# An attention and mixture-of-experts layer on one core: a unit's near tables written by one transfer and read by one, in place of six of half units

## What is computed

```python
scores = jnp.einsum('bhqd,bhkd->bhqk', q, k) / scale
rel = build_relative_position(S, S, BUCKETS, MAX_REL)        # log buckets of q - k
c2p = jnp.take_along_axis(jnp.einsum('bhqd,hpd->bhqp', q, pos_k), clip(rel + ATT_SPAN), axis=-1)
p2c = jnp.take_along_axis(jnp.einsum('bhkd,hpd->bhkp', k, pos_k), clip(-rel + ATT_SPAN), axis=-1)
scores = scores + (c2p + swapaxes(p2c, -1, -2)) / scale
probs = jax.nn.softmax(scores, axis=-1)
ctx = jnp.einsum('bhqk,bhkd->bhqd', probs, v)
```

## Time and profile before

| | us |
|---|---|
| median of 3 runs | 1870.73 (1870.19 to 1876.4) |
| the profiled execution's own time | 1863.67 |
| its span, first to last instruction | 1861.8 |
| PE busy | 1708.2 (92%) |
| DVE busy | 1417.6 (76%) |
| ACT busy | 1163.0 (62%) |
| POOL busy | 1057.3 (57%) |
| mean granted TensorE clock | 0.919 of full speed |

### The profile page before, as it was taken

How to read it: one execution, slowest core, us unless ns; L and a number is a source line. 1 busy time by engine, 2 the same in 40 slices (tenths; PEclk the granted TensorE clock), 3 DMA queues, 4 the chain that set the end, 5 groups by cost and what they waited for, 6 DMA issues and landing times. The chain is left out here.

```text
span 1861.8 us, 41287 instructions
## 1 busy us (share of the span) xinstructions
PE 1708.2 (92%) x13752; PEld 1164.0 (63%) x13752; DVE 1417.6 (76%) x4111; ACT 1163.0 (62%) x2784; POOL 1057.3 (57%) x1260
## 2 busy tenths in 40 slices
PE   7953899999999999999999999999869967999997
PEld 4531565666666666666666666666435656999996
DVE  4751898999999999999999999999534453555553
ACT  6843577788887888888888888787613441222221
POOL 0002777777777777877778777788214321333332
PEclk9985899999999999999999999999955566999998
DMA  5976787878778887788887877877065424666662
GB/s 152 302 259 214 250 277 261 278 256 284 263 257 296 267 276 262 268 285 267 278 276 253 288 260 264 274 262 244 19 169 182 139 74 137 208 189 201 201 198 68
DMA packets 297313, 426.33 MB, mean 229 GB/s; under 512 B 35773, under 2 KB 238545, under 8 KB 297008
## 3 DMA queue, kind: packets, MB, share of 16 engines
q1 hardware_dynamic: 285764, 393.28, 64.7%
q10 hardware_dynamic: 7596, 21.10, 3.6%
q0 software_dynamic: 3744, 9.31, 1.4%
HBM read 245.85 MB, written 178.05 MB: 228 GB/s over the span
## 5 line engine op out<-in xcount | busy, mean ns | idle before, releaser
L839 ACT ACTIVATE t_probsT<-t_flip 128x512 f32<-128x512 f32 x1024 | 626.0, 614 | 201.8 <-PE t_flip L735 148.0
L785 DVE TENSOR_REDUCE t_most<-t_scores 128x1 f32<-128x640 f32 (+1 forms) x512 | 435.0, 850 | 82.1 <-PE t_scores L712 78.8
L804 DVE TENSOR_SCALAR t_band<-t_band,t_top 128x384 f32<-128x384 f32 (+1 forms) x512 | 413.9, 809 | 0.0
L749 PE MATMUL t_sum_ps<-t_probsT,t_vals 128*32 128x256 f32 x4096 | 327.7, 392 | 0.2 <-ACT t_probsT L839 0.2
L831 ACT COPY t_table<-t_table_ps 128x388 f32<-128x388 f32 x512 | 247.9, 484 | 56.3 <-issue 29.0
L916 POOL TENSOR_TENSOR t_near<-t_near,masks 128x768 f32<-128x768 f32 (+1 forms) x128 | 273.5, 2137 | 0.0
L789 DVE CUSTOM_DVE_ANT_0 t_band<-t_scores,t_near 128x384 f32<-128x384 f32 (+1 forms) x512 | 261.6, 511 | 0.0
L735 PE MATMUL t_flip<-masks,t_band 128*128 128x128 f32 x1408 | 261.1, 274 | 0.0
L712 PE MATMUL t_scores<-masks,t_near 128*128 128x128 f32 x1408 | 241.8, 275 | 5.0 <-POOLq L919 5.0
L705 PE MATMUL t_scores<-t_afters,t_quests 105*128 105x256 bf16 (+3 forms) x1024 | 244.0, 288 | 1.3 <-DVE t_most L789 1.3
L900 POOL TENSOR_TENSOR t_near<-t_near,masks 128x384 f32<-128x384 f32 (+1 forms) x128 | 147.1, 1149 | 124.1 <-DMA t_near<-skew_d 117.5
(11 more groups left out here) (194 smaller groups left out, 2670.2 us busy)
## 6 DMA issues: line engine op xcount, KB each, us to landing
skew_d<-t_table SPq DMA_DIRECT2D x128, 1024.0 KB, 9.3
t_near<-skew_d SPq DMA_DIRECT2D x128, 640.0 KB, 8.1
t_near<-skew_d SPq DMA_DIRECT2D x128, 384.0 KB, 7.3
e_w<-in_L_ffn_W_dram ACTq DMA_DIRECT2D x39, 512.0 KB
e_w<-in_L_ffn_W_dram SPq DMA_DIRECT2D x39, 512.0 KB
split_d<-p_part SPq DMA_DIRECT2D x32, 384.0 KB, 3.3
t_afters<-split_d SPq DMA_DIRECT2D x128, 96.0 KB
t_quests<-split_d SPq DMA_DIRECT2D x128, 96.0 KB
```

The lines of the kernel that those rows point to most:

```text
L749: last = nc.tensor.matmul(sum_ps[32 * g:32 * g + 32, 0:2 * P], vals[b % 2][:, j, h * VDIM:h * VDIM + 32], probsT[s % 3][:, g * 2 * P:(g + ...
L785: nc.vector.tensor_reduce(most[:, c, 1:2], out[:, wide:S], AX.X, ALU.max)
L804: nc.vector.tensor_scalar(band[n % 2][:, t, 0:wide], band[n % 2][:, t, 0:wide], top[n % 2][:, t:t + 1], None, ALU.subtract).then_inc(level ...
L839: nc.scalar.activation(probsT[s % 3][:, half * 512:(half + 1) * 512], flip_ps[half][:, :], ACT.Exp, scale=SCALE).then_inc(expd, 1)
```

## The change

The two halves of a unit's tables become one piece: one write of 2048 KB, one read of 2048 KB. `table` in SBUF is laid out so that a partition's 16 KB are contiguous, as they are in HBM. In SP's loop the read of unit u+1 comes first, then the loads, then the write of unit u+2. The read waits for the whole unit of two before (`scored`, `seen`) and for the whole write. `edge` waits for the one read; its steps are issued later in the loop. `load_vals(0)` and the clearing of `spent` semaphores move to later rounds of SP's loop. The constant rows go out in three transfers over all six buffers, on one semaphore.

```diff
-            def skew_write(n, h):
-                sp.wait_ge(table_kept, n * QT + 4 * h + 4)
+            def skew_write(n):
+                sp.wait_ge(table_kept, n * QT + QT)
                 if n >= 2:
-                    sp.wait_ge(skew_in[n % 2][0], 16 * 2 * (n // 2))
-                    sp.wait_ge(skew_in[n % 2][1], 16 * 2 * (n // 2))
-                sp.dma_start(view(skew_d, n % 2 * (P * PITCH) + h * 4 * SPOT + 1, [[PITCH, P], [TABLE, 2], [1, 4 * SPOT]]),
-                             table[n % 2][:, h, :, :, :].rearrange("p a u v -> p a (u v)")).then_inc(skew_out[n % 2][h], 16)
-
-            def skew_read(n, h):
+                    sp.wait_ge(skew_in[n % 2], 16 * (n // 2))
+                sp.dma_start(view(skew_d, n % 2 * (P * PITCH) + 1, [[PITCH, P], [1, PITCH]]),
+                             table[n % 2][:, :, :, :].rearrange("p a u v -> p (a u v)")).then_inc(skew_out[n % 2], 16)
+
+            def skew_read(n):
                 if n >= 2:
-                    sp.wait_ge(scored, (n - 2) * QT + 4 * h + 4)
-                    sp.wait_ge(seen, (n - 2) * QT + 4 * h + 4)
-                sp.wait_ge(skew_out[n % 2][h], 16 * (n // 2 + 1))
-                lo, hi = PIECES[h]
-                for tab in range(2):
-                    sp.dma_start(near[n % 2][:, tab, lo:hi, P:W3],
-                                 view(skew_d, n % 2 * (P * PITCH) + tab * TABLE + lo * SPOT + P,
-                                      [[PITCH - 1, P], [SPOT, hi - lo], [1, SPOT]])).then_inc(skew_in[n % 2][h], 16)
+                    sp.wait_ge(scored, (n - 1) * QT)
+                    sp.wait_ge(seen, (n - 1) * QT)
+                sp.wait_ge(skew_out[n % 2], 16 * (n // 2 + 1))
+                sp.dma_start(near[n % 2][:, :, :, P:W3].rearrange("p a u v -> p (a u) v"),
+                             view(skew_d, n % 2 * (P * PITCH) + P, [[PITCH - 1, P], [SPOT, 2 * QT], [1, SPOT]])
+                             ).then_inc(skew_in[n % 2], 16)
...
             for u in range(-4, N + 3):
-                if 0 <= u + 2 < N:
-                    skew_write(u + 2, 0)
                 if 0 <= u + 1 < N:
-                    skew_read(u + 1, 1)
+                    skew_read(u + 1)
                 if 0 <= u + 4 < N:
                     load_unit(u + 4)
                 if 0 <= u + 2 < N and u % FARS == 0:
                     load_far(u + 2)
-                if u == -4:
+                if 0 <= u + 2 < N:
+                    skew_write(u + 2)
+                if 0 <= u - 2 < N:
+                    store(u - 2)
+                if u == -1:
                     load_vals(0)
+                if u == 1:
                     for semaphore in spent:
                         sp.sem_clear(semaphore)
-                if 0 <= u + 2 < N:
-                    skew_write(u + 2, 1)
-                    skew_read(u + 2, 0)
-                if 0 <= u - 2 < N:
-                    store(u - 2)
...
-                if u % 4 == 0 and n >= 2:
-                    act.wait_ge(skew_out[n % 2][h], 16 * (n // 2))
-                    act.wait_ge(side_kept, (n - 2) * 2 + h + 1)
-                wide = table[n % 2][:, h, :, u % 4, :]
+                if u == 0 and n >= 2:
+                    act.wait_ge(skew_out[n % 2], 16 * (n // 2))
+                    act.wait_ge(side_kept, (n - 2) * 2 + 2)
+                wide = table[n % 2][:, :, u, :]
...
-            for i in range(BUFS):
-                for dst, src in ((quest[i][KROWS:FAR, :], ones[0:3, :]), (after[i][FAR:ROWS, :], after_rows[:, :]),
-                                 (before[i][FAR:ROWS, :], before_rows[:, :])):
-                    nc.scalar.dma_start(dst, src).then_inc(rows_set[i], 16)
+            for dst, src in ((quests[KROWS:FAR, :, :], ones[0:3, :]), (afters[FAR:ROWS, :, :], after_rows[:, :]),
+                             (befores[FAR:ROWS, :, :], before_rows[:, :])):
+                nc.scalar.dma_start(dst, src.unsqueeze(1).to_broadcast([dst.shape[0], BUFS, S])).then_inc(rows_set, 16)
...
-            steps = ((8, 1, (3,)), (9, 1, (4,)), (1, 0, (0, 1)), (2, 0, (2,)), (3, 0, (3,)), (4, 0, (4,)),
-                     (5, 1, (0, 1)), (6, 1, (2,)))
+            steps = ((8, 1, (3, 4)), (3, 0, (0, 1)), (4, 0, (2,)), (5, 0, (3,)), (6, 0, (4,)), (7, 1, (0, 1, 2)))
```

More of the change, by code:

```diff
@@ L532, in attend @@
     PITCH = 2 * TABLE
-    PIECES = ((0, 3), (3, QT))
     EDGES = ((0, 3), (3, QT - 1))
@@ L550, in attend @@
         vals = [sb(f"vals{i}", [P, QT, VROW]) for i in range(2)]
-        table = [sb(f"table{i}", [P, 2, 2, 4, SPOT]) for i in range(2)]
+        table = [sb(f"table{i}", [P, 2, QT, SPOT]) for i in range(2)]
         side = [sb(f"side{i}", [P, 2, QT]) for i in range(3)]
@@ L568, in attend @@
         before_set, ident_made, twin_made = sem("t_before_set"), sem("t_ident_made"), sem("t_twin_made")
-        rows_set = [sem(f"t_rows_set{i}") for i in range(BUFS)]
+        rows_set = sem("t_rows_set")
         hats_in = [sem(f"t_hats_in{i}") for i in range(BUFS)]
@@ L573, in attend @@
         vals_in = [sem(f"t_vals_in{i}") for i in range(2)]
-        skew_out = [[sem(f"t_skew_out{i}{h}") for h in range(2)] for i in range(2)]
-        skew_in = [[sem(f"t_skew_in{i}{h}") for h in range(2)] for i in range(2)]
+        skew_out, skew_in = ([sem(f"t_{w}{i}") for i in range(2)] for w in ("skew_out", "skew_in"))
         ctx_out = [sem(f"t_ctx_out{i}") for i in range(2)]
@@ L695, in score @@
                     pe.wait_ge(ident_made, 1)
-                if t == 0 and n < BUFS:
-                    pe.wait_ge(rows_set[n], 16 * 3)
+                if s == 0:
+                    pe.wait_ge(rows_set, 16 * 3)
                 if t == 0:
@@ L823, in keep_table @@
                 n, u = x // QT, x % QT
-                h = u // 4
                 act.wait_ge(table_made, x + 1)
-                if u % 4 == 0 and n >= 2:
-                    act.wait_ge(skew_out[n % 2][h], 16 * (n // 2))
-                    act.wait_ge(side_kept, (n - 2) * 2 + h + 1)
-                wide = table[n % 2][:, h, :, u % 4, :]
+                if u == 0 and n >= 2:
+                    act.wait_ge(skew_out[n % 2], 16 * (n // 2))
+                    act.wait_ge(side_kept, (n - 2) * 2 + 2)
+                wide = table[n % 2][:, :, u, :]
                 ends = view(wide.tensor, wide.offset, [list(wide.ap[0]), list(wide.ap[1]), [SPOT - LEFT, 2], [1, LEFT]])
@@ L887, in keep_side @@
                     pool.wait_ge(edge_made, (n - 3) * 10 + 10)
-                nc.gpsimd.tensor_copy(side[n % 3][:, :, 4 * h:4 * h + 4], table[n % 2][:, h, :, :, BAND]).then_inc(side_kept, 1)
+                nc.gpsimd.tensor_copy(side[n % 3][:, :, 4 * h:4 * h + 4], table[n % 2][:, :, 4 * h:4 * h + 4, BAND]).then_inc(side_kept, 1)
             def edge(n, h, step):
@@ L898, in edge @@
                 if step == 0:
-                    pool.wait_ge(skew_in[i][h], 16 * 2 * (n // 2 + 1))
+                    pool.wait_ge(skew_in[i], 16 * (n // 2 + 1))
                     nc.gpsimd.tensor_tensor(head[:, 0, :, :], tail[:, 0, :, :], above, ALU.mult).then_inc(edge_made, 1)
```

## The result

The changed kernel takes 2004.09 us (median of 4 runs, 2000.2 to 2009.89), beside 1870.46 for the kernel before in the same comparison. The ratio is 1.071 (95%: 1.0675 to 1.0744), a loss of 134 us. The forecast was 1968: the sign and the mechanism hold, the size is 36 us short.

What follows compares the result with a forecast made beforehand. PE was taken to set the pace, 17.8 us a unit. Steady loop +104, start -1, stall -6 gave +97 on the profiled 1863.67, 1961, and 7 more to the median, 1968 us; range 1880 to 2150, its core 1900 to 2030.

Steps and rivals of the forecast that it cites:

- Two signs of being wrong: Signs listed against the forecast: period 17.8 with the read released by `seen`; write over 9 us; PE clock under 1.0.
- The two loops nearly agree; the larger rules.: Steady attention: loaded engines' loop 19.6 us a unit, loop through POOL and PE 19.2; the first sets the pace.
- that is where PE will stand: PE waits for tiles 3 to 7's tables, 1.8 us a unit in one or two pieces.
- The clock: Rival: PE's new stops lower its clock in each unit, 58 x 1.7 us, about 2065 us; chance 0.07.
- The growth: Steady attention: units grow from 17.8 to 19.6 us, 1.8 more over 58 units, +104 us.
- The loaded engines' loop: Three DMA engines: write 5.1, gap 2.8, read 5.5, loads 5.9, far loads 0.3, together 19.6 us a unit.
- The 1 us of slack on these engines: Before the change, the three loaded DMA engines work 16.8 us of each 17.8, with 1 us to spare.
- the rival of no loss: Rival: the loaded engines' loop stays below 17.8 us a unit; start and stall are gained, 1860 us; chance 0.12.
- The start: First table copy on ACT about 9 us sooner, first near products about 175; net -1 us.
- The stall of before: PE's stop of 3.51 us at 293 us and its lowered clock do not come on top: -6 us.
- Large pieces are slow: Rival: the write in 16 KB pieces moves 211 GB/s and takes 9.9 us, 2246 us in all; chance 0.18.
- a short gap: Rival: a gap of 1.2 to 1.5 us gives 18.1 to 18.4 us a unit, 1880 to 1900; chance 0.08.

Runs made afterwards that it cites:

- e10: The changed kernel with 6 unused products on PE ahead of `turn_top`, filling only the second of its two stops: 1993.82 us, ratio 1.066.
- e7: The changed kernel with eight buffers for queries and keys in place of six: 1931.05 us, ratio 1.0343.
- e5: The kernel before with an unused fifth load of 96 KB in each unit: 1955.63 us, ratio 1.0471.
- e2: The kernel before with only the constant rows changed, three transfers in place of eighteen: 1867.62 us, ratio 0.9986.
- e3: The changed kernel with each of a unit's four loads cut in three, to use all 16 engines: 2013.24 us, ratio 1.0786.
- e1: The changed kernel with the write of unit u+2 issued ahead of the round's loads: 1871.87 us, ratio 1.0018.
- e9: The kernel before with loads behind writes and reads, constant rows in three transfers, `load_vals(0)` and the clearing of `spent` later: 1860.93 us, ratio 0.9962.

## Why the prediction was right, and where its size was off

**The sign and the argument hold.** The read is issued when its own write lands (SP's wait of 384.6 us in 39 times from 450 to 1250 us); in 3 of these 39 the scores on PE came last, by 0.8 us in all; between a write and its read no other table transfer is queued, and right after the loads' issue the DMA share is 0.10, then 0.24 from 677 to 680 us, where about 3/16 were forecast. That was to show the forecast right, and it does. PE stops with POOL as releaser, ahead of the near products and of `turn_top`, which was a sign of being right. Two signs of being wrong stayed away (a period of 17.8, a slow write) and one came: the clock is under 1.00 in the attention's windows (0.95).

**The step that failed: "The two loops nearly agree; the larger rules."** I worked out 38.4 us for two units through POOL and PE, 39.2 through the loaded engines, and took the latter. The chain of two units measures 41.6 in the pair shown and 41.0 on average, term by term:

| | forecast | this pair | mean of 18 |
|---|---|---|---|
| read issued to POOL's start | 8.2 | 9.6 | 9.4 |
| POOL's edges | 14.2 | 14.1 | 14.1 |
| end of the edges to the next loads | 1.9 | 3.7 | 3.2 |
| loads to the landing of the write | 14.1 | 14.2 | 14.3 |

Two terms were mis-sized. The landing of a read was priced as start and bytes of a lone transfer; it takes 1.2 us more on average. And PE's part was taken at the pace of a PE that never stops (1.4 us from the near products to the loads); it takes 1.3 us more on average.

**The place where PE stands was wrong too.** I had it wait for the second half of the edges, at tile 3 ("that is where PE will stand"). It never did. It waits for the first half at tile 0, then for `split_top`, and reaches tile 3 only 1.8 us after the edges have ended. That this cost the sum so little is luck: at full clock the way through `split_top` is 0.3 us longer than the forecast's way through tile 3 (2.2 in e10, 1.9 forecast).

**The clock.** I had its fall as a rival (0.07), by one stop of 3.51 us, and wrote that my stops were shorter. Shorter ones were enough: behind the stops of 2.49 and 1.43 us, with 3.2 us of work between them (663.31 to 666.54), it is down to 0.51, and the same work takes 1.5 us more. In other units a single stop did it. Behind one of 2.69 us the clock is 0.50 at once:

```profile
826.38 0.69 PE L705 MATMUL t_scores<-masks,t_near 128*128 128x128 f32 x2 [2.69 <-POOLq L910]
```

```profile
827.00:830.00 3.00, 3.00 (x19) 1.83 (x19) 1.73 (x6) 1.23 (x4) 2.92 (x5) 0.50 0.09 36
```

And behind stops of 2.75 and 1.42 us (ending at 581.91 and 586.56) it stays at 1.00. What decides between these cases is not shown. The rival's price was wrong as well: I had 97 us for it, and holding the clock up (e10) gives back about 10.

**The growth.** 58 units at 1.8 were to be 104 us; it is 151.7, 56 at 2.7. That is the profiled execution, whose span grew by 146.3 (2008.1 against 1861.8); it is the longest of the four, and the medians lie 134 apart. That 2004 lies inside the forecast's 1900 to 2030 is partly luck, since those bounds were worked out from the gap in the loaded engines' loop, and the other loop was the longer one. (By its own terms the upper bound, 20.8 a unit, gives 2038 and not 2030.) **The loaded engines' loop**, 19.6 a unit, could not be seen in the changed kernel, but in e7, where the chain is opened, units are 19.0 apart: inside the bounds of 18.1 to 20.8. The 1 us of slack on these engines, on which the rival of no loss rested, was not there before the change either (e5).

**The start.** ACT's first copy at 144.00 (forecast 144.2), the first near products at 176.62 (about 175), 3 us sooner than before: the gain was to be 4 there and 1 later. Right in direction and small, as e2 says too.

**The stall of before**, -6 us, cannot be told apart any more: the changed kernel has stops of that kind in every second unit.

**Large pieces are slow** (0.18) is ruled out: with the last of the loads beside it the write moves 412 GB/s in 680 to 685 us, and with next to none 430 (e3), where 4 KB pieces went at 410. The 211 GB/s of the earlier trace rows belong to that load, not to long pieces. **No loss** (0.12) and **a short gap** (0.08) fail at the period of 20.5.

**The skill's rule.** The Trainium skill, page "DMA: Bandwidth & Descriptors", section "Rules for kernel authors", wants small transfers merged. Taken alone that is harmless here (e1, with the same 2 MB transfers, is 0.2% from the kernel before), but it did not gain either: the six transfers, of 0.4 to 1 MB, already moved 380 to 410 GB/s. e9, with the smaller ones, is the fastest.

## What to carry to other kernels

Where a queue is worked in order, ask what stands between a write and the read that waits for it, before asking how large they are: merging six transfers into two took away the one that kept the queue filled, and moving the write ahead of the loads gave nearly all of it back. When loads wait for a buffer that a later consumer frees, follow the chain over as many units as there are until it closes, and add up its terms at the durations of a stalled unit. An edit that puts the producer's transfer first in a round is cheap to try; here the old kernel with it, and with the constant rows in three transfers, became 0.4% faster (e9). When a chain is written down, check of each link that something really waits there: PE was held by `split_top`, not by the edges behind it.

## What the runs showed of the hardware

A write in pieces of 16 KB went at 430 GB/s (e3, 658 to 662 us), no slower than 4 KB pieces at 410.

Two stops of PE, 2.49 and 1.43 us with 3.2 us of work between, were followed by a stretch at the lower of the clock's two levels, 1.2 GHz (0.51 from 669 to 672 us). So was a single stop of 2.69 us (0.50 from 827 to 830 us), and two of 2.75 and 1.42 us were not (1.00 from 587 to 593 us). With the second stop filled (e10) the mean clock was 1.00 over 800 us; the first was still there in 19 units, but shorter, 0.9 us on average.

Loads of 0.39 MB that by their DMA share of 0.22 run on about three of the 16 engines held back a write queued behind them on all. While it was still under way the share was 0.16 (663 to 666 us). The times: from issue to the next read 11.5 us for 2 MB behind the loads, 8.8 for 1 MB, and 6.8 for 2 MB when the same loads were cut in three (e3).
